# A recurrent stage that trains its own weights: token norms rooted on twelve partitions, two first token products in one, first rates first, and four new engine orders

## The reference, cut to what matters

```python
def newtonschulz5(G, steps=2):
    a, b, c = (3.4445, -4.775, 2.0315)
    X = G.astype(jnp.bfloat16)
    X = X / (jnp.linalg.norm(X, axis=(1, 2), keepdims=True) + 1e-07)   # one norm per matrix
    for _ in range(steps):
        A = X @ X.transpose(0, 2, 1)
        Bm = b * A + c * (A @ A)
        X = a * X + Bm @ X
    return X

def step(carry, inp):                     # per chunk; carry: w0, w1, w2, 128 x 128 each
    gate = ki @ w0_;  hb = ki @ w2_;  sg = silu(gate);  hidden = sg * hb
    dhidden = vi @ w1_.transpose(0, 2, 1)
    dhbm = dhidden * sg;  dgba = silu_backprop(dhidden * hb, gate)
    w1g = newtonschulz5(einsum(hidden * lr1i, vi))
    w0g = newtonschulz5(einsum(ki * lr0i, dgba))
    w2g = newtonschulz5(einsum(ki * lr2i, dhbm))
    w0_, w1_, w2_ = each (w + wg), its columns scaled back to their first norms
    oi = silu(qi @ w0_) * (qi @ w2_) @ w1_
```

## Time and profile before

| | |
|---|---|
| median of 3 runs | 1576.62 us (1576.53 to 1580.05) |
| the profiled execution | 1579.73 us, of which the span of its instructions is 1578.0 us |
| busy over the whole span | PE 92%, DVE 80%, ACT 64%, POOL 55% |
| the recurrent stage | first token product at 149.47 us, the 32 roots of token norms from 167.18 to 782.09 us |

### The profile page before, as it was taken

One profiled execution on the slowest core, in us unless ns is written; L12 is line 12 of the kernel. 1 busy time (PEld: TensorE's weight loads), 2 busy tenths in 40 slices (PEclk: granted clock), 3 DMA queues, 4 the chain that ended last, 5 costly groups with the idle time before them and its releaser, 6 DMA issues. The chain is left out here.

```text
span 1578.0 us, 44161 instructions
## 1 busy us (share of the span) xinstructions
...
## 2 busy tenths in 40 slices
...
GB/s 121 257 237 172 113 121 160 148 174 177 193 178 176 173 159 93 99 95 115 87 91 158 158 199 203 195 205 213 194 196 210 196 199 199 189 72 107 264 267 136
DMA packets 264982, 264.40 MB, mean 168 GB/s; under 512 B 87467, under 2 KB 236312, under 8 KB 264752
## 3 DMA queue, kind: packets, MB, share of 16 engines
...
...
## 5 line engine op out<-in xcount | busy, mean ns | idle before, releaser
L1749 POOL DMA_INDIRECT scratch_y<-eo,goes x224 | 225.8, 1008 | 340.5 <-ACT eo L1843 294.0
L1774 PE MATMUL e_psGU<-wexp,e_xT 128*64 x896 | 291.2, 468 | 0.2 <-issue 0.2
L1776 PE MATMUL e_psGU<-e_up,e_xT 128*64 128x352 f32 x896 | 291.1, 468 | 0.0
L1381 POOL DMA_INDIRECT scratch_buf<-rows,dest x180 | 194.5, 1080 | 49.1 <-issue 39.7
L1864 ACT ACTIVATE e_up<-wexp 128x704 f32 x224 | 177.0, 790 | 26.9 <-issue 26.9
L1774 PEld LDWEIGHTS e_psGU<-wexp,e_xT 128*64 128x64 f32 x896 | 114.0, 137 | 122.4 <-issue 122.4
L1984 DVE COPY e_down<-wexp 128x512 f32 x224 | 93.9, 419 | 92.9 <-PE e_psD L1799 89.6
L1843 ACT ACTIVATE eo<-e_psD 128x256 f32<-128x256 f32 x224 | 85.5, 384 | 87.2 <-issue 46.7
L1391 POOL TENSOR_TENSOR f_wnr<-f_wss,f_half 128x4 f32<-128x4 f32 x96 | 98.5, 1035 | 59.0 <-DVE f_wss L1194 58.5
L1832 ACT ACTIVATE e_sgm<-e_psGU 128x176 f32<-128x176 f32 x224 | 71.1, 318 | 78.5 <-PE e_psGU L1776 64.6
L1793 PE MATMUL e_psD<-wexp,e_hT 112*64 x448 | 115.5, 379 | 1.6 <-DVE e_hT L1939 1.6
...
## 6 DMA issues: line engine op xcount, KB each, us to landing
...
```

Of the source, the lines that this page charges most:

```text
L1381: pool.indirect_dma_start(out=T["buf"], out_offset=bass.IndirectOffsetOnAxis(dest[:, i, k:k + 1], 0), in_=rows[:, i % RR, :], in_offset=No ...
L1749: pool.indirect_dma_start(out=T["y"], out_offset=bass.IndirectOffsetOnAxis(goes[:, n:n + 1], 0), in_=eo[:, n % OB, :], in_offset=None, bou ...
L1774: pe.matmul(psGU[0:RT, n % 2, 0:2 * F], xT[:, n % 4, k, 0:RT], ring[:, bass.ds(at[n] + k * 2 * F, 2 * F)], start=(k == 0), stop=(k == KD - 1))
L1776: mm = pe.matmul(psGU[RT:P, n % 2, 0:2 * F], xT[:, n % 4, k, RT:P], up2[:, n % 2, k * 2 * F:(k + 1) * 2 * F], start=(k == 0), stop=(k == K ...
```

## The change

It has five parts.

1. Norms: `totals` swaps its operands (row sums as weights, one column of ones moving) so that the twelve totals lie on twelve partitions, one each. The cast, the power and the added 1e-7 then handle 12 x 1 numbers. The reciprocal reads that one number per partition and writes it 128 times (12 x 128). A new stage `spread` transposes this by TensorE into 128 x 12, DVE copies it to `r` and forms `r2`. The third `gram` waits for `r2`.
2. `gate` and `hidden_base` become `gates`: four matmuls of 256 columns (W0 and W2) with one semaphore. It waits for both weights. `slope` writes to another PSUM bank, `token_hid` and `token_dg` read the new place, `grads_0` also waits for `hid`.
3. `rate(0, 0)` and `rate(1, 0)` stand ahead of the root of the first weights' norms on POOL.
4. `first_norms` moves from `token_hid` to behind `squares(0, 0, 2)`.
5. The four orders are new.

```diff
-            def gate(x, it):
+            def gates(x, it):
                 if it:
-                    pe.wait_ge(wnd[x].sem, wnd[x].at(it - 1, W0 + 1))
+                    pe.wait_ge(wnd[x].sem, wnd[x].at(it - 1, W2 + 1))
                 pe.wait_ge(k_in[x].sem, k_in[x].at(it, 8))
-                token_product(prod[:, x, W0, 0:D], weights(x, it)[0][W0], 0, x).then_inc(tg[x].sem, 1)
+                for h in range(H):
+                    for b2 in range(2):
+                        dst = prod[CH * b2:CH * b2 + CH, x, W0, :].rearrange("p (m c) -> p m c", m=2)
+                        both = first[:, W0:W1, 2 * b2 + h, :] if it % NC == 0 else Wn[:, W0:W1, x, 2 * b2 + h, :]
+                        mm = pe.matmul(dst[:, :, h * HD:(h + 1) * HD], kvT[:, x, h, b2, :], both, start=True, stop=True)
+                mm.then_inc(tg[x].sem, 1)
-            def hidden_base(x, it):
...
             def totals(x, it):
                 pe.wait_ge(rsc[x].sem, rsc[x].at(it, 1))
-                pe.matmul(prod[:, x, 2, 32:32 + M], ones_f[:, :], rowsq[:, x, :], start=True, stop=True).then_inc(totp[x].sem, 1)
+                pe.matmul(prod[0:M, x, 2, 32:33], rowsq[:, x, :], ones_f[:, 0:1], start=True, stop=True).then_inc(totp[x].sem, 1)
+
+            def spread(x, it):
+                pe.wait_ge(rd[x].sem, rd[x].at(it, 2))
+                pe.transpose(prod[:, x, 2, 64:64 + M], rw[:, x, :], identf[0:M, 0:M]).then_inc(totp[x].sem, 1)
...
                 if m == 2:
-                    pe.wait_ge(ssd[x].sem, ssd[x].at(it, 1))
+                    pe.wait_ge(rd[x].sem, rd[x].at(it, 4))
...
-                v.reciprocal(r[:, x, :], nb[:, x, :]).then_inc(rd[x].sem, 1)
-                v.wait_ge(rd[x].sem, rd[x].at(it, 2))
+                v.reciprocal(rw[:, x, :], nb[:, x, 0:1].broadcast_to([M, P])).then_inc(rd[x].sem, 1)
+
+            def spread(x, it):
+                v.wait_ge(totp[x].sem, totp[x].at(it, 2))
+                v.tensor_copy(r[:, x, :], prod[:, x, 2, 64:64 + M]).then_inc(rd[x].sem, 1)
+                v.wait_ge(rd[x].sem, rd[x].at(it, 3))
...
             def root(x, it):
                 pool.wait_ge(ssd[x].sem, ssd[x].at(it, 1))
-                pool.tensor_tensor(nb[:, x, :], ssb[:, x, :], half[:, :], ALU.pow).then_inc(n1[x].sem, 1)
+                pool.tensor_tensor(nb[:, x, :], ssb[:, x, :], half[0:M, 0:1], ALU.pow).then_inc(n1[x].sem, 1)
```

More of the change, by code:

```diff
@@ L475 @@
 PE_ORDER = (
[L476 to L490, removed]
@@ L491 @@
-    ("read", 1, 1, 0), ("turn_x", 0, 2, 1), ("back", 0, 0, 0), ("gram", 1, 0, 2), ("back", 0, 0, 1),
+    ("x2", 1, 1, 0, 1), ("x2t", 1, 1, 1), ("gates", 0, 0), ("x2t", 1, 1, 2), ("x2", 1, 1, 1, 1), ("gram2", 1, 1, 0),
+    ("gram2", 1, 1, 1), ("output", 1, 2, 0), ("hidden_back", 0, 0), ("poly2", 1, 1, 0), ("x2", 1, 1, 2, 0),
+    ("poly2", 1, 1, 1), ("last", 1, 1, 0), ("back", 0, 1, 2, 1), ("gram2", 1, 1, 2), ("turn_o", 0, 2, 0),
+    ("last", 1, 1, 1), ("grads_0", 0, 0), ("grads_1", 0, 0), ("grads_2", 0, 0), ("grads_3", 0, 0),
@@ new lines @@
+    ("project", 0, 2, 0), ("poly2", 1, 1, 2), ("row_sums", 0, 0), ("turn", 0, 0, 0, 1), ("turn", 0, 0, 1, 0),
+    ("totals", 0, 0), ("last", 1, 1, 2), ("turn", 0, 0, 2, 1), ("gram", 0, 0, 0), ("read", 0, 1, 0),
+    ("turn_x", 1, 3, 1), ("spread", 0, 0), ("back", 1, 1, 0), ("gram", 0, 0, 1), ("back", 1, 1, 1),
+    ("logits", 1, 3, 1), ("gram", 0, 0, 2), ("poly", 0, 0, 0), ("poly", 0, 0, 1), ("poly", 0, 0, 2), ("x2t", 0, 0, 0),
+    ("x2", 0, 0, 0, 1), ("x2t", 0, 0, 1), ("gates", 1, 0), ("x2t", 0, 0, 2), ("x2", 0, 0, 1, 1), ("gram2", 0, 0, 0),
@@ new lines @@
+    ("gram2", 0, 0, 1), ("output", 0, 1, 0), ("hidden_back", 1, 0), ("poly2", 0, 0, 0), ("x2", 0, 0, 2, 0),
+    ("poly2", 0, 0, 1), ("last", 0, 0, 0), ("back", 1, 1, 2, 1), ("gram2", 0, 0, 2), ("turn_o", 1, 2, 0),
+    ("last", 0, 0, 1), ("grads_0", 1, 0), ("grads_1", 1, 0), ("grads_2", 1, 0), ("grads_3", 1, 0),
+    ("project", 1, 2, 0), ("poly2", 0, 0, 2), ("row_sums", 1, 0), ("turn", 1, 0, 0, 1), ("turn", 1, 0, 1, 0),
+    ("totals", 1, 0), ("last", 0, 0, 2), ("turn", 1, 0, 2, 1), ("gram", 1, 0, 0), ("read", 1, 1, 0),
@@ L506 @@
 )
 DVE_ORDER = (
[L509 to L517, removed]
-    ("update", 0, 0, 0), ("update", 0, 0, 1), ("row_norms", 0, 0, 0), ("row_norms", 0, 0, 1), ("squares", 1, 0, 0),
@@ L519 @@
-    ("squares", 1, 0, 1), ("squares", 1, 0, 2), ("gate_x", 1, 2, 0), ("factors", 0, 0, 0), ("row_sums", 1, 0),
-    ("renorm", 0, 0, 0), ("totals", 1, 0), ("norm_x", 1, 2), ("factors", 0, 0, 1), ("pick", 1, 3),
-    ("update", 0, 0, 2), ("renorm", 0, 0, 1), ("norms", 1, 0), ("a", 1, 0, 0), ("a", 1, 0, 1), ("a", 1, 0, 2),
+    ("place", 1, 4), ("rows_x", 1, 3), ("gate", 0, 0), ("slope", 0, 0), ("token_hid", 0, 0), ("slope_2", 0, 0),
+    ("both", 0, 0), ("token_dg", 0, 0), ("update", 1, 1, 0), ("token_dhb", 0, 0), ("update", 1, 1, 1),
@@ new lines @@
+    ("row_norms", 1, 1, 0), ("row_norms", 1, 1, 1), ("squares", 0, 0, 0), ("factors", 1, 1, 0), ("squares", 0, 0, 1),
+    ("squares", 0, 0, 2), ("gate_x", 0, 2, 0), ("factors", 1, 1, 1), ("row_sums", 0, 0), ("renorm", 1, 1, 0),
+    ("norm_x", 0, 2), ("totals", 0, 0), ("update", 1, 1, 2), ("pick", 0, 3), ("norms", 0, 0), ("renorm", 1, 1, 1),
+    ("row_norms", 1, 1, 2), ("spread", 0, 0), ("a", 0, 0, 0), ("a", 0, 0, 1), ("a", 0, 0, 2), ("b", 0, 0, 0),
+    ("b", 0, 0, 1), ("factors", 1, 1, 2), ("b", 0, 0, 2), ("read", 0, 1, 0), ("place", 0, 3), ("rows_x", 0, 2),
@@ new lines @@
+    ("gate", 1, 0), ("slope", 1, 0), ("token_hid", 1, 0), ("slope_2", 1, 0), ("both", 1, 0), ("token_dg", 1, 0),
+    ("update", 0, 0, 0), ("token_dhb", 1, 0), ("update", 0, 0, 1), ("row_norms", 0, 0, 0), ("row_norms", 0, 0, 1),
+    ("squares", 1, 0, 0), ("factors", 0, 0, 0), ("squares", 1, 0, 1), ("squares", 1, 0, 2), ("gate_x", 1, 2, 0),
+    ("factors", 0, 0, 1), ("row_sums", 1, 0), ("renorm", 0, 0, 0), ("norm_x", 1, 2), ("totals", 1, 0),
+    ("update", 0, 0, 2), ("pick", 1, 3), ("norms", 1, 0), ("renorm", 0, 0, 1), ("row_norms", 0, 0, 2),
@@ L522 @@
+    ("spread", 1, 0), ("a", 1, 0, 0), ("a", 1, 0, 1), ("a", 1, 0, 2), ("b", 1, 0, 0), ("b", 1, 0, 1),
+    ("factors", 0, 0, 2), ("b", 1, 0, 2), ("read", 1, 1, 0),
 )
 POOL_ORDER = (
[L525 to L527 removed]
```

69 lines of the change are left out of this document (36 added, 33 removed), and 20 rows, old and new, of the table ACT_ORDER.

## The result

The changed kernel takes 1569.54 us (median of 4 runs, 1567.59 to 1571.36) against 1576.69 for the kernel before (4 runs beside it); ratio 0.9953, 95% interval 0.9941 to 0.9965. It became faster by 0.47%, 7 us; forecast was 7 us slower.

A forecast was written before the change was run, and what follows sets the result against it. DVE was taken to bound 25 half steps: +0.76 - 0.83 + 0.44 = +0.37 us each, +9.5 in all; with the start's -2.4, +7.1 on 1576.62 gives 1583.7 us. Range for 8 in 10: 1564 to 1597.

The forecast's parts named there:

- The reciprocal: Token norms on DVE: the reciprocal at 128 elements per partition takes 0.93 us, its pitch becoming 0.85 instead of 0.26.
- row_norms1: DVE's second row sum waits for ACT's `square1`, which comes behind a2-2; it starts 0.31 us late.
- squares0: DVE's first square waits for x0, behind `o_keep` on ACT; it starts 0.17 us late.
- the gates' 0.31 us on PE: Merged gate products on PE take 1.17 us for 1.48, saving one entry and exit; PE gains 0.31.
- The first half steps are PE's and nothing: Half steps before POOL sends rows: PE's sequence binds, so the change brings nothing, bounds of 0.3 us each.
- update0: DVE's first update starts 8.95 us after the start of A0, 0.24 late for PE's `last0`; `update1` 0.07 late.
- the norms: Token norms on DVE: longer reciprocal plus the copy out of `spread` add 0.76 us per half step.
- place: Router's multiply on DVE: the new order avoids the hold-up by POOL's renorm multiply, -0.83 us per half step.
- the two old ones: Old DVE stalls at `row_norms0` (0.21 us) and the three squares (0.15 us) go, leaving net +0.44 of stalls.
- factors0: On DVE between the squares: its root from POOL is ready, 12.37 against 12.57, so no stall.
- half of the stalls: Rival for steady half steps: 19.76 us each, only the start's gain remains, about 1574 us, no change; chance 0.20.
- The start: Earlier rates and moved `first_norms`: gradients 5.6 us earlier, first A net -2.4 us, once; bounds -5.6 and 0.

The follow-up runs named there:

- c_old_norms: The changed kernel with the old twelve-column norms back (no `spread`, root of 128 x 12), all orders new; 1587.83 us, ratio 1.0067.
- a_start_undone: The changed kernel with only the old start put back (rates behind the first weights' root, `first_norms` inside `token_hid`); 1571.1 us, ratio 0.9961.
- i: The kernel before, in its old orders, with the new norms and `spread` put in; 1598.47 us, ratio 1.013.
- h: The changed kernel with the merged gate products split into two adjacent ones of 128 columns; 1569.41 us, ratio 0.9943.
- j: The changed kernel with `hidden_back` on PE put back behind the second polynomial's first lot; 1583.25 us, ratio 1.0037.
- g: The changed kernel with ACT's `square1` ahead of a2-2, straight behind `square0`; 1579.02 us, ratio 1.0007.
- k: The version d with `output` and `hidden_back` moved straight behind `gates` on PE; 1592.56 us, ratio 1.0093.
- d: The changed kernel with a one-element reciprocal and a 12x12 diagonal spread by a product with ones, replacing the 128-wide reciprocal; 1553.82 us, ratio 0.9847.
- f: The changed kernel with `place` straight behind `factors2` in DVE's order; 1591.3 us, ratio 1.0093.
- b: The kernel before with the new start alone, old norms, gates and orders; 1572.74 us, ratio 0.9972.
- m: The kernel before with `hidden_back` on PE moved ahead of the second polynomial's first lot, behind `output`; 1574.66 us, ratio 0.9983.
- e: The kernel before with `rows_x` and `place` moved behind `token_hid` in DVE's order; 1592.01 us, ratio 1.0091.

## Why the prediction was wrong

Two steps of the prediction failed. With the steady half steps as they were measured (-0.6 us over 25 of them instead of +9.5), and all else as forecast, the sum of +7.1 becomes -3.0 us; with the first six as measured (-6.0 instead of nothing) it becomes +1.1. So the error in the steady half steps is the larger, and alone turns the sign; the first half steps bring the sum to the size that was measured.

**Steps that held.** The reciprocal at 0.94 us (forecast 0.93), the root at 0.57 (0.58), L1290 at 0.225 in the median (0.22), the first gradients at 154.48 (154.5), `row_norms1` 0.28 late (0.31), `squares0` 0.16 late (0.17), the gates' 0.31 us on PE (before two groups of 0.149 + 0.385 + 0.205 us from matmul to matmul, after one of 0.149 + 0.705 + 0.312). The Trainium skill's repeat count of 8 (VectorE: DVE Perf Modes, section Walkthrough: the 8-slice pipeline in each mode) had been read as 1.2 us for the reciprocal; the row says 941 ns, and from 32 to 128 elements 594 / 96 = 6.2 ns each. The measurement decides, and the prediction had gone by the rows.

**The failed step ahead of the steady state: "The first half steps are PE's and nothing (bounds of 0.3 each)."** They gave 6.0 us, 1.5 in the first and 3.1 in the second; the four behind them gave 0.2 to 0.5 each. PE's groups from the first A to the seventh with idle time in front (last two numbers: idle us, and what ended most of it), first of the kernel before:

```profile
L868 PE MATMUL prod<-f_A,f_beta_i 128*128 128x512 bf16 x18 | 7.8, 436 | 8.4 <-DVE f_A L1181 8.3
```

then of the changed one:

```profile
L874 PE MATMUL prod<-f_gamma_r,f_gamma_l 128*128 128x512 bf16 x36 | 14.5, 403 | 0.8 <-DVE f_A L1194 0.5
...
L862 PE MATMUL prod<-ident,f_rw 12*128 12x12 f32 x6 | 1.4, 227 | 1.6 <-DVE f_rw L1182 1.6
```

and of c_old_norms:

```profile
L870 PE MATMUL prod<-f_A,f_beta_i 128*128 128x512 bf16 x18 | 7.6, 422 | 7.3 <-DVE f_A L1187 7.3
L917 PE MATMUL prod<-ident,f_WT 128*128 128x128 f32 x48 | 7.6, 280 | 4.3 <-DVE f_WT L1213 4.3
```

PE alone wasn't the bound there. It stood 8.4 us at the first polynomial and waited for A, that is for the chain from row sums over totals, root and reciprocal, in which the long root is 2.3 us; after, 0.8 there and 1.6 at `spread`. The forecast looked for waits between 400 and 700 us only, where DVE is the bound and the root is hidden, and took a window with PE at 96% for a full one. In that window the changed kernel is indeed only 0.5 us faster in two half steps. The first two half steps, which the forecast did not look at, had PE at 83% (34.96 of 42.10).

The clock has a part that was not separated. In the kernel before, PE stood idle for 2.37 us until 193.60 us, and from 194.7 to 198.1 its granted clock was 0.50, the level of 1.2 GHz; in the changed kernel it stays at 1.00 from 173.0 us to the end of the stage's half steps. The version a_start_undone has such a fall too (188.7 to 192.1 us; its second half step takes 18.26 us instead of 17.55) and is early at 112.3 all the same, and c_old_norms has none and takes 116.4, so the clock isn't the main cause.

Undone one at a time, the early stretch reads: new orders with the old root 116.4 (c), new norms in the old orders 120.3 (i), both 112.8, the start undone 112.3 (a), the gates split 112.9 (h). So it is the short root together with the orders: the new norms are worth 3.6 us in the new orders, and in the old ones they make the stretch 1.5 us longer. Of the orders `hidden_back` is 1.7 to 1.9; the start has no part in it in the new orders. How much each other move of the orders gives was not separated.

**The failed step in the steady state: `update0` at a + 8.95 and `update1` behind it, 0.31 us of stalls.** They are absent: `update0` starts at a + 8.68. The forecast took out of PE's way what had moved from ahead of `last0`, but priced `hidden_back`'s move ahead of `poly2` at nothing. It puts two groups of 64-column products side by side and fills a wait of PE. Without these stalls the sum per half step is 0.79 (the norms, by the measured pitches of reciprocal and copy) - 0.83 (`place`) + 0.44 (the stalls that are there, 0.28 and 0.16) - 0.36 (the two old ones) = +0.04, and with the 0.12 at `factors0`, whose root the forecast had ready, +0.16; measured is -0.03 (19.79 to 19.76). The 0.19 left over were not traced to one place. With the stalls, in j, the half step is 20.16 where 20.15 was forecast. That shows the mechanism, but the hit to 0.01 is luck: the stalls at the updates are 0.45 us there, not 0.31, and other terms made up for it. The forecast's rival "half of the stalls", 19.76, was right about the steady state. It missed the early half steps too, and so stood at 1574.

**Terms off in size.** The start: first A 3.9 us earlier, not 2.4. The squares ended at 158.8, not 159.8, and the rest of the chain took 0.5 us less than written (root of the norms done at 165.4, not 166.5).

**Not seen at all.** From the last A to the last keys the changed kernel takes 2.9 us more. The new orders, made for the steady state, may cost there, where no token work stands beside the last tiles, but the versions don't show it cleanly. With new orders the stretch takes 63.7 (c), 64.3 (a), 64.4 (g), 64.9 (k), 65.2 (d), 65.8 (h), 65.9 (f) and 66.4 us (j); with old ones 61.7 (b), 62.9 (m), 63.2 (i) and 66.1 (e). The granted clock is a rival that was left untested: its mean in the stretch is 0.63 before and 0.59 after, it is 0.59 or 0.60 in h and j, which take long too, and 0.66 in a, c, g and k, whose orders are new and whose times lie 0.9 to 2.2 us lower; but f has 0.66 as well and takes 65.9. So the cause stays open. The last 2.0 us, in the stages behind, vary between 725.6 and 729.5 over these versions with no edit in them; what sets them stays open too.
